# Encoder start-up: embedding rows gathered one job ahead, two weight loads issued later, and products of zeros on TensorE ahead of the first job

## The reference, cut to what matters

```python
B, D, H, L, F, V = 8, 256, 16, 4, 1024, 7500      # x is (8, 256) token numbers
h = emb[x] + pos_encoding                          # row gather from HBM
for l in range(4):
    y = layer_norm(h)
    q, k, v = split_heads(y @ attn_w[l, :3] + attn_b[l, :3])
    p = softmax(q @ k.T * dk**-0.5)
    h = h + (p @ v) @ attn_w[l, 3] + attn_b[l, 3]
    h = h + relu(layer_norm(h) @ w1[l] + b1[l]) @ w2[l] + b2[l]
```

## Time and profile before

| | |
|---|---|
| Median of 3 runs | 2105.56 us (2102.9 to 2107.07) |
| The profiled execution | 2102.53 us, of which the span is 2100.7 us |
| TensorE busy | 2037.0 us (97%) |
| VectorE, ScalarE, GpSimd busy | 62%, 49%, 10% |
| DMA | 69.84 MB, mean 33 GB/s |
| Mean granted TensorE clock | 0.993 |

### The profile page before, as it was taken

How to read it: one execution, slowest core, us unless ns; L and a number is a source line. 1 busy time by engine, 2 the same in 40 slices (tenths; PEclk the granted TensorE clock), 3 DMA queues, 4 the chain that set the end, 5 groups by cost and what they waited for, 6 DMA issues and landing times. The chain is left out here.

```text
span 2100.7 us, 42201 instructions
## 1 busy us (share of the span) xinstructions
PE 2037.0 (97%) x16462; PEld 1657.2 (79%) x16462; DVE 1299.0 (62%) x3344; ACT 1031.9 (49%) x3525; POOL 215.8 (10%) x251
## 2 busy tenths in 40 slices
PE   5899999999999999999999999899999999999998
PEld 4688888888888888888888877678788788877776
DVE  4676767676676776766767863767777646423322
ACT  3666656656566565666656552545445531111111
POOL 4000000000000000000000000000000000234444
PEclk9999999999999999999999999999999999999999
DMA  6000000100000400000000000500000100025542
GB/s 182 1 1 2 1 2 2 69 1 2 1 2 1 155 2 2 2 2 1 2 2 2 2 1 1 183 1 1 1 1 1 61 1 11 24 78 165 156 142 65
DMA packets 27203, 69.84 MB, mean 33 GB/s; under 512 B 9920, under 2 KB 17825, under 8 KB 23680
## 3 DMA queue, kind: packets, MB, share of 16 engines
q1 hardware_dynamic: 18432, 59.42, 8.4%
q0 software_dynamic: 6400, 5.63, 1.1%
q10 hardware_dynamic: 2176, 2.10, 0.3%
HBM read 61.16 MB, written 17.40 MB: 37 GB/s over the span
## 5 line engine op out<-in xcount | busy, mean ns | idle before, releaser
L547 ACT ACTIVATE probs<-bank,nmax 128x256 f32<-128x256 f32 x1024 | 474.4, 478 | 413.1 <-DVE nmax L716 413.1
L716 DVE TENSOR_REDUCE nmax<-bank 128x2 f32<-128x512 f32 x512 | 317.9, 683 | 208.6 <-PE bank L401 205.4
L414 PE MATMUL bank<-ident,probs 128*128 128x128 f32 x2048 | 271.9, 276 | 5.1 <-DVE pts L724 5.1
L414 PEld LDWEIGHTS bank<-ident,probs 128*128 128x128 f32 x2048 | 232.6, 141 | 39.7 <-DVE pts L724 22.5
L446 PE MATMUL bank<-yT,weights 128*128 128x256 f32 x1024 | 248.3, 386 | 0.9 <-ACT aT L570 0.9
L458 PE MATMUL bank<-weights,aT 128*128 128x256 f32 x1024 | 232.6, 380 | 1.3 <-DVE h L754 0.8
L547 ACT ACTIVATION_READ_ACCUMULATOR probs<-bank,nmax 128x1 f32 x1024 | 216.0, 211 | 0.0
L446 PEld LDWEIGHTS bank<-yT,weights 128*128 128x128 f32 x1024 | 184.5, 190 | 37.7 <-ACT aT L570 11.6
L458 PEld LDWEIGHTS bank<-weights,aT 128*128 128x128 f32 x1024 | 189.5, 190 | 25.3 <-DVE h L754 1.2
L724 DVE COPY pts<-bank 128x512 f32<-128x512 f32 x256 | 172.8, 675 | 38.6 <-PE bank L414 38.5
L556 ACT ACTIVATE pts<-bank 128x512 f32<-128x512 f32 x256 | 156.8, 612 | 21.4 <-PE bank L414 18.7
(11 more groups left out here) (218 smaller groups left out, 2935.4 us busy)
## 6 DMA issues: line engine op xcount, KB each, us to landing
wqkv<-in_experts SPq DMA_DIRECT2D x16, 1024.0 KB
weights<-in_wtok SPq DMA_DIRECT2D x4, 2048.0 KB, 19.0
wqkv<-in_experts SPq DMA_DIRECT2D x16, 512.0 KB
expert_rows<-xT_all SPq DMA_DIRECT2D x10, 546.0 KB, 16.5
xrows<-expert_rows SPq DMA_DIRECT2D x16, 273.0 KB
weights<-in_wtok SPq DMA_DIRECT2D x3, 1024.0 KB
wqkv<-in_wqkv SPq DMA_DIRECT2D x1, 3072.0 KB, 17.5
weights<-in_shared SPq DMA_DIRECT2D x1, 3072.0 KB, 10.8
```

The source lines that it names most:

```text
L414: last = pe.transpose(g[:, (NT * x + kb) * P:(NT * x + kb + 1) * P], p[:, x, kb * P:(kb + 1) * P], ident[:])
L547: last = nc.scalar.activation(probs[u % 8][:, x, :], g[:, x * S:(x + 1) * S], ACT.Exp, bias=nmax[j % 2][:, col:col + 1], accum_out=rsum[j ...
L716: nc.vector.tensor_reduce(nmax[j % 2][:, col:col + 2], g[:].rearrange("p (x s) -> p x s", x=2), AX.X, ALU.max, negate=True).then_inc(s_max, 1)
```

## The change

Five parts. (1) On SP, the load of layer 0's feed-forward weights waits for job 0's k result instead of the second gather, and the loads of layer 1 wait for job 0's last feed-forward result instead of nothing. (2) On GpSimd, both first roots come ahead of any further gather; the gathers and position additions of sequence j + 2 then stand inside job j, between that job's two roots. (3) On TensorE, seven products of zeros (128x128 by 128x512, into bank 6, which holds nothing yet) stand ahead of the first transposes: five behind the zeroing of `v[0]` and the arrival of the constants, one behind the gather of sequence 0, one behind its statistics. (4) Two more stand in job 0, group 1, between the second turn of the probabilities and `y_T(1)`. (5) On VectorE, `v[0]` is zeroed ahead of the wait for the token numbers.

```diff
+        s_zero = sem("e_zero")
...
-            sp.wait_ge(s_gather[1], 16 * NT)
+            evacuated(sp, (0, "k"))
             sp.dma_start(weights[0][:, 2048:], io["wtok"][0, :, 2048:]).then_inc(s_wf[0], 16)
             for l in range(1, L):
-                if l >= 2:
-                    evacuated(sp, ((l - 1) * B - 1, "down", 1))
+                evacuated(sp, ((l - 1) * B - 1 if l >= 2 else 0, "down", 1))
...
             root(1, 0)
-            gather(range(2 * NT, 3 * NT))
             root(1, 1)
-            gather(range(3 * NT, B * NT))
-            for s in range(2, B):
-                positions(s)
             for j in range(JOBS + 1):
                 if real(j + 1) and j > 0:
                     root(1, j + 1)
+                if j + 2 < B:
+                    gather(range((j + 2) * NT, (j + 3) * NT))
+                    positions(j + 2)
...
+            def idle(n, x=0):
+                z = v[x][:].rearrange("p i n x d -> p (i n x d)")
+                for _ in range(n):
+                    pe.matmul(bank[6][:], z[:, 0:P], z[:, 512:1024], start=True, stop=True)
+
+            pe.wait_ge(s_zero, 1)
+            idle(5)
+            pe.wait_ge(s_gather[0], 16 * NT)
+            idle(1)
+            pe.wait_ge(s_var[0], 1)
+            idle(1)
             y_T(0)
...
                     turn_probs(jp, cp, 1)
+                    if (j, c) == (0, 1):
+                        idle(2, 1)
...
+            step = Tally(s_step, 0)
+            nc.vector.memset(v[0][:], 0.0).then_inc(s_zero, 1)
             dve.wait_ge(s_idx, 16)
-            step = Tally(s_step, 0)
...
-            for x in range(2):
-                step.up(nc.vector.memset(v[x][:], 0.0))
+            step.up(nc.vector.memset(v[1][:], 0.0))
```

## The result

The changed kernel takes **2097.4 us** (median of 5 runs, 2094.71 to 2098.94) beside 2105.56 us (5 runs, 2102.9 to 2107.07): 0.9963, interval 0.9949 to 0.9978. On a second chip, in 12 runs against 35, the ratio is 0.9981 (0.9971 to 0.999). The gain is real, and its size less certain than the first pair says: the medians there, 2096.54 and 2101.52, are 5.0 us apart, those of the first chip 8.2.

A forecast was written before the change was run, and what follows sets the result against it. TensorE, 97% busy, was taken as the bound, so start-up shifts carry through. Terms -1.9 - 3.6 - 1.8 + 0.4 + 0.5 = -6.4 from 2102.53 gave 2096.1 us, plus half of 3.0 us: 2097.5 us, range 2092 to 2104.

The forecast's parts named there:

- the half of 3.0 us: Added to the sum because the profiled execution was 3.0 us under the median of the runs, giving 2097.5 us.
- Start products: Seven products of zeros ahead of the first transposes raise TensorE's clock early: -1.9 us net, from -2.5 to +4.4.
- the prediction's other reading: Transposes don't count as activity for TensorE's clock; the zeros lift it at about 8.3 us and the start term is -2.5.
- the 6.5 us of the sum: Time taken from TensorE's first work to the clock's rise at the start, putting the rise at 10.7 us.
- `v[0]` zeroed early: On VectorE, 0.9 us inside its 1.27 us wait for the token numbers: nothing; without that cover 0.9 us at most.
- Two loads later: With the moved gathers, frees DMA in job 0 so VectorE's late release comes on time: -3.6 us, bounds 0 and -3.85.
- the "remote" waits: VectorE's waits of 0.85 and 3.00 us in job 0, read as a late release in a stretch of busy DMA.
- the port rule: GpSimd can't write gather descriptors while VectorE holds the shared port in some copy modes; at most 0.3 us seen.
- Clock from 34 to 44 us: Without TensorE's 4 us idle ahead of `y_T(1)`, `pv` and scores run at full clock: -1.8 us, bounds 0 and -2.5.
- The pair in job 0: Two products of zeros ahead of `y_T(1)`, 1.94 us at full clock, mostly inside a wait: +0.4 us, bounds 0 and +2.1.
- Gathers and additions in jobs: Between GpSimd's two roots in jobs 1 to 5, 7.3 us of the 9.77 us are used, 2.5 us left: 0.
- Later stretches: Further half-clock stretches of TensorE in jobs 0 and 1, as many expected: +0.5 us, from -4 to +3.

The follow-up runs named there:

- `before_again`: The kernel before, unchanged, run again on the second chip for a second profile: 2101.11 us, 1.0004.
- `after_again`: The changed kernel, unchanged, run again on the same chip as its variants: 2096.54 us (12 runs).
- `start_products_only`: The kernel before with only the seven products of zeros at the start and the early zeroing of `v[0]`: 2097.38 us, 0.9988.
- `additions_later`: The kernel before with only GpSimd's six position additions moved, one per job instead of a block; gathers and loads as before: 2099.43 us, 0.9991.
- `loads_only`: The kernel before with only the two weight loads later, gathers all at the start as before: 2100.81 us, 1.0004.
- `gathers_only`: The kernel before with only the gathers and position additions moved into the jobs, loads as early as before: 2099.16 us, 0.9991.
- `moves_only`: The kernel before with both loads and gathers moved as in the change, no products of zeros: 2098.91 us, 0.9989.
- `no_pair`: The changed kernel without the two products of zeros in job 0: 2097.21 us, 0.9984 of the kernel before.

## Why the prediction was right, by its own steps

**Time and sign.** Forecast 2097.5 (2092 to 2104; the sum itself gives 2097.6), measured 2097.4. The shift at the start was forecast as -6.4 us and read as -6.4 at job 2; that both agree to a tenth is luck, as the next points show (the second pair of profiles, `before_again` and `after_again`, has 91.46 and 85.80 us there, 5.7). The total is luck too: the half of 3.0 us that was added for the gap to the median stands in for the 2.2 us given back late, and against the medians of the second chip the gain is 5.0 us, not the 8.1 that the forecast makes against 2105.56.

**Start products, forecast -1.9.** The first two profiles differ by 2.3 us, but one pair says little: without the products the first scores come at 21.70 to 23.89 us in six profiles (mean 22.6), with seven products at 19.91 to 21.81 in six (mean 20.9). That is 1.7 us. The mechanism is right: durations of one record fall from 977 ns and more to 592 ns inside the seven products, in two stretches of the changed kernel:

```profile
L485 PE MATMUL bank<-v x7: 977/1061/1219, 4.2 to 9.5; 128*128 128x512 f32 x7
...
L485 PE MATMUL bank<-v x7: 592/592/593, 10.3 to 12.9; 128*128 128x512 f32 x7
```

The change of speed lies between 9.5 and 10.3 us, which is the forecast's 10.7 within a microsecond. But this profile is the latest of eight: in the seven others that begin with such products the first record at full speed starts at 7.7 to 9.4 us, nearer the 8.3 of the prediction's other reading, by which transposes don't count. Its question can now be answered by rows. From the first of the seven products to the first record at full speed it is 3.5 to 6.1 us in those eight profiles. In the six without them it is 3.0 to 6.4 us from the first q product and 5.3 to 8.7 from the first transpose. The first two ranges agree; counting from the transposes, as the 6.5 us of the sum did, gives more. Six and eight profiles support that reading and don't prove it.

The clock does not have to stay up, though. Windows 15 to 19 us of `start_products_only`:

```profile
15.00:19.00 4.00, 3.75 (x10) 3.02 (x11) 0.25 (x1) 0.20 (x1) 3.14 (x4) 0.59 1.01 400
```

The clock fell again beneath the q products (5.41 us for 3.72) in three of the six profiles that have seven products, and in neither of the two with an eighth. In those two it fell at 25.1 and 26.5 us instead. The forecast had no term for that.

**`v[0]` zeroed early, forecast 0.** Right: VectorE still waits 0.45 us for the token numbers behind the zeroing.

**Two loads later, forecast -3.6 together with the gathers.** The size is right: 10.25 - 6.89 = 3.4 us. The cause is wrong. The later loads brought nothing, and the traffic alone doesn't make the release late: three profiles with the same loads and gathers (`before_again`, `additions_later`, `start_products_only`) have no such wait. In two profiles a gather issue and the block of additions behind it held VectorE for 4.1 and 5.3 us. In the profile that was read, 3.85 us are the "remote" waits, whose cause stays open, and 0.75 us is the block (some 1.4 of these 4.6 us only use up the wait for scores that VectorE has there in the changed kernel); whether the change had any part in their going is not shown. So the -3.6 is right for this pair of executions, and what the moves bring on average is nearer the 2.6 us between `loads_only` and `gathers_only`. The prediction cites the port rule in one direction alone, VectorE holding up a gather, finds 0.3 us and drops it. The direction that cost in those two was the other one, and the row for it, `den` at 31.00 us with 0.92 us where 0.17 is usual, stood in the timeline of before, unread, behind a larger wait whose label drew the eye.

**Clock from 34 to 44 us, forecast -1.8.** Right in size: `pv` 1.08 for 1.94 and scores 1.15 for 2.09. The reason given, that TensorE no longer idles for 4 us, doesn't hold: without that idle time the scores of group 2 still took 2.09 us in `moves_only`, `gathers_only`, `additions_later` and `no_pair`, and 2.02 in `start_products_only`. In the changed kernel the clock was low from 27.3 to 30.7 us, beneath the turns and the pair, so the fall had moved. What decides where it comes stays open.

**The pair in job 0, forecast +0.4.** Too small: 0.96 us, between the bounds of 0 and 2.1. The step that failed is its duration: it was priced at full clock and ran mostly at half in both profiles.

**Gathers and additions in jobs, forecast 0.** Right. GpSimd in job 1 of the changed kernel, which answers to the earlier trace rows:

```profile
60.56 1.01 POOL L297 DMA_INDIRECT h<-in_emb,idxu  x1 [0.19 <-issue]
61.87 0.96 POOL L297 DMA_INDIRECT h<-in_emb,idxu  x1 [0.30 <-issue]
65.40 1.28 POOL L310 TENSOR_TENSOR h<-h,pe_sb 128x512 f32<-128x512 f32 x1 [2.57 <-DMA h<-in_emb,idxu]
70.39 0.72 POOL L306 TENSOR_TENSOR sd<-mv,half 128x2 f32<-128x2 f32 x1 [3.71 <-DVE mv L682]
```

3.71 us to spare where 2.5 were expected, and 3.38, 3.41, 3.03 and 3.38 in the four jobs behind it. The addition falls beside VectorE's maxima, which it doesn't hold up (2.48 us for four).

**Later stretches, forecast +0.5.** About right up to 85 us: -2.3 at the start, -3.4 to the first maximum of group 1, -1.8 for `pv` and scores and +1.0 for the pair make -6.5, of -6.4 measured, so 0.1 is left for this term. The text looked no further, and the 2.2 us beyond 1240 us are the same kind of event.

## What to carry to other kernels

When a small VectorE operation on SBUF alone lasts longer than its siblings, read GpSimd's row at its end before blaming traffic: a block of additions is one long hold here, and one addition per job beside the maxima is none. A test of such a collision counts only if the two would have met without the edit: work out from the first scores when `den` comes before calling a clean profile a proof. A product put into a wait of TensorE costs what sticks out of it, and up to double at half clock: hold the end of the copy beside its end. With a gain of 0.2 to 0.4% from a start-up, look at places in the profile and at a dozen runs each: every execution carries falls of the clock of its own, and one profile can't tell them from the edit.

## What was not expected of the hardware

- A `tensor_scalar` on 128x2 elements took 4.26 and 5.49 us when it came during a gather issue with back-to-back GpSimd additions of 1.2 us each behind it, instead of 0.17: it did not get in between two of them.
- A gather issue held the same operation for 0.1 us (0.28 us), ending within 0.01 us of it.
- Products of zeros and of constants lift the clock alike: the first record at full speed starts at 8.5 to 10.3 us with zeros (four profiles) and at 7.7 to 9.4 with constants (four).
- The "remote" waits of 0.85 and 3.00 us appear in one of two profiles of the same kernel and in none of the twelve others. What they were stays open. So does what decides whether the clock falls again near 15 us: an eighth product went with none in two profiles of two, but three of six did without it as well.
